# Eight slots instead of nine in the second attention's weighing, and another share of the softmax sums

## What is computed

```python
q = layernorm(q_x, ln_q_g, ln_q_b) @ Wq.T
kv = layernorm(kv_x, ln_kv_g, ln_kv_b) @ Wkv.T
attn = softmax(einsum('bhqd,bhkd->bhqk', q, k) * scale)
out = einsum('bhqk,bhkd->bhqd', attn, v)
x = q_x + out @ Wo.T + bo
h = silu(x @ W1.T + b1)
x = x + h @ W2.T + b2
```

## Time and profile before

| | us |
|---|---|
| three runs, median (lowest to highest) | 5529.31 (5528.18 to 5532.56) |
| the profiled execution | 5531.83 |
| its span, first to last instruction | 5529.7 |
| busy: TensorE / VectorE / ScalarE / GpSimd | 5310.5 / 4009.0 / 3173.3 / 2329.5 |
| mean granted TensorE clock | 0.977 of full |

### The profile page before, as it was taken

One profiled execution on the slowest core, in us unless ns is written; L12 is line 12 of the kernel. 1 busy time (PEld: TensorE's weight loads), 2 busy tenths in 40 slices (PEclk: granted clock), 3 DMA queues, 4 the chain that ended last, 5 costly groups with the idle time before them and its releaser, 6 DMA issues. The chain is left out here.

```text
span 5529.7 us, 93901 instructions
## 1 busy us (share of the span) xinstructions
PE 5310.5 (96%) x28684; PEld 3343.9 (60%) x28684; DVE 4009.0 (72%) x6947; ACT 3173.3 (57%) x5792; POOL 2329.5 (42%) x1156
## 2 busy tenths in 40 slices
PE   8989999999699799999999999999999996999999
PEld 7744444444377466666666666666666663787777
DVE  6589999999577688888888888888888885332331
ACT  4258888888433366666666666666666664322222
POOL 0000000000000388888888888888888885000000
PEclk9989999999899799999999999999999998999999
DMA  7521111111343311111111111111111111322220
GB/s 216 129 46 37 39 38 38 38 38 32 112 120 111 102 41 29 40 41 41 36 34 39 42 41 35 34 40 42 41 32 36 41 30 61 114 92 69 92 84 23
DMA packets 329591, 324.44 MB, mean 59 GB/s; under 512 B 185744, under 2 KB 193808, under 8 KB 327184
## 3 DMA queue, kind: packets, MB, share of 16 engines
q1 hardware_dynamic: 329232, 319.92, 21.8%
HBM read 219.18 MB, written 100.53 MB: 58 GB/s over the span
## 5 line engine op out<-in xcount | busy, mean ns | idle before, releaser
L426 DVE TENSOR_REDUCE a_maxes<-a_mscore 128x1 f32<-128x458 f32 (+4 forms) x5376 | 3037.8, 625 | 599.0 <-PE a_mscore L485 566.9
L409 ACT ACTIVATE a_prob<-a_score 128x512 f32<-128x512 f32 x4992 | 2635.7, 598 | 1184.4 <-PE a_score L494 1171.2
L494 PE MATMUL a_score<-a_q,a_k 97*128 97x512 f32 (+1 forms) x4992 | 1975.6, 430 | 11.6 <-ACT a_prob L409 7.9
L485 PE MATMUL a_mscore<-a_k,a_qm 96*128 96x458 f32 (+4 forms) x5376 | 1892.3, 415 | 53.7 <-DMA a_k<-k 52.4
L513 PE MATMUL a_acc<-a_prob,a_v 128*32 128x512 f32 x9984 | 1593.6, 601 | 0.0
L485 PEld LDWEIGHTS a_mscore<-a_k,a_qm 96*128 96x128 f32 (+1 forms) x5376 | 1475.0, 310 | 177.0 <-issue 54.0
L375 POOL TENSOR_TENSOR a_added<-a_added,a_prob 128x1024 f32<-128x1024 f32 x640 | 1527.3, 2386 | 71.0
L494 PEld LDWEIGHTS a_score<-a_q,a_k 97*128 97x128 f32 (+1 forms) x4992 | 916.0, 193 | 966.5 <-ACT a_prob L409 524.8
L372 POOL TENSOR_TENSOR a_added<-a_prob 128x1024 f32<-128x1024 f32 x128 | 305.1, 2383 | 1893.5 <-ACT a_prob L409 1879.6
L508 PE MATMUL a_acc<-a_prob,a_ones 128*1 128x512 f32 x2048 | 960.9, 591 | 0.0
L513 PEld LDWEIGHTS a_acc<-a_prob,a_v 128*32 128x32 f32 x9984 | 291.8, 108 | 297.7 <-issue 153.2
(11 more groups left out here) (205 smaller groups left out, 3878.0 us busy)
## 6 DMA issues: line engine op xcount, KB each, us to landing
a_qm<-q SPq DMA_DIRECT2D x384, 64.0 KB, 1.9
a_q<-q SPq DMA_DIRECT2D x384, 64.0 KB, 1.9
acc<-a_acc_sb SPq DMA_DIRECT2D x384, 64.0 KB
e_part<-acc SPq DMA_DIRECT2D x90, 256.0 KB, 3.4
a_k<-k SPq DMA_DIRECT2D x48, 416.0 KB, 6.2
q<-m_qout SPq DMA_DIRECT2D x128, 128.0 KB, 2.3
e_wo<-wo_split SPq DMA_DIRECT2D x32, 512.0 KB, 4.1
k<-kv_k1out SPq DMA_DIRECT2D x24, 512.0 KB, 2.9
```

The costliest lines, as they stand in the source:

```text
L409: act.activation(prob[:, t], score[SCORES[it.j][t]][:], ACT.Exp, scale=SCALE).then_inc(exp_done, 1)
L426: dve.tensor_reduce(maxes[j][:, t, c:c + 1], mscore[u % UNIT_BANKS][:, 0:wide], AX.X, ALU.max).then_inc(unit_read, 1)
L485: pe.matmul(mscore[u % UNIT_BANKS][:, 0:wide], qm[j][r:r + ROW, t:NB:NB // P], kt[kk][r:r + ROW, at:at + wide], start=True, stop=True).the ...
L494: pe.matmul(score[SCORES[it.j][t]][:], kt[it.k][r:r + C, i * P:(i + 1) * P], qt[it.j][r:r + C, :], start=True, stop=True).then_inc(score_d ...
```

## The change

- Slots 0 and 1 of an item now hold four value tiles (tiles 0 to 7). Slots 2 to 7 hold three value tiles (8 to 25) and in column 3 a sum: tiles 8, 9, 23, 24, then `rest`, which is the two real rows of tile 25 by `ones[0:2]`, then `total`. That is eight slots in four batches, behind t = 10, 12 (previous item), 17 and 22.
- Column 3 now has two contents in an item: values of batch 0, then sums from batch 1. So ScalarE copies the values of column 3 to a new buffer `side` at t = 20 (`copy_side`), batch 1 waits for that, and SP stores it as a fourth part.
- VectorE adds up tiles 1 to 7, in four pieces of 128 columns (each a strided reduction of 128 by 7 by 128), at t = 8, 10, 12 and 21 of the same item. Piece 0 waits for all of GpSimd's adds of the item before.
- GpSimd adds tiles 0 and 10 to 11 and 12, then pairs 13 to 22: six adds from tile 12's exponential on. The two-row add goes.
- `acc` is copied out at t = 13. The units per tile follow another table.
- `ending` loads and adds four parts. To make room for that, `total` is kept in `h[1]` and some reciprocals in `h[0]`.

```diff
-            self.ROWS, self.SIDE, self.SUMS = 128, 3, 1
-            self.slots = [[(0, 3 * i), (1, 3 * i + 1), (2, 3 * i + 2), (3, ("one", 3 * i))] for i in range(8)]
-            self.slots.append([(0, 24), (1, 25), (3, ("sum", None))])
-            self.batches = [[0, 1], [2, 3], [4, 5], [6, 7], [8]]
-            self.at = {3: (3, True), 9: (4, True), 14: (0, False), 19: (1, False), 25: (2, False)}
-            self.copy_at = 5
+            self.ROWS, self.SIDE, self.SUMS = 128, 4, 1
+            self.slots = [[(c, 4 * i + c) for c in range(4)] for i in range(2)]
+            for i in range(2, 8):
+                first = 8 + 3 * (i - 2)
+                what = [("one", 8), ("one", 9), ("one", 23), ("one", 24), ("rest", 25), ("sum", None)][i - 2]
+                self.slots.append([(0, first), (1, first + 1), (2, first + 2), (3, what)])
+            self.batches = [[0, 1], [2, 3], [4, 5], [6, 7]]
+            self.at = {10: (2, True), 12: (3, True), 17: (0, False), 22: (1, False)}
+            self.copy_at, self.side_at = 13, 20
+            self.sum_at = (8, 10, 12, 21)
...
-            more = dict(enumerate([2, 1, 1, 0, 1, 2, 1, 1, 1, 0, 1, 2, 1, 1, 1, 1, 1, 2, 1, 1, 1, 1, 2, 1, 1, 0]))
+            more = dict(enumerate([1, 2, 1, 0, 2, 0, 1, 2, 1, 1, 0, 2, 0, 1, 1, 2, 1, 1, 1, 1, 2, 1, 1, 2, 0, 1]))
...
-ADDS = 9
-ON_VECTOR, PIECES = range(22, 25), 4
-READ_BY = 7
+ADDS, READ_BY, SUMS_READ = 8, (1, 2, 5, 6), 8
+ON_VECTOR, PIECES = (range(1, 8),), 4
+VSUMS = len(ON_VECTOR) * PIECES
...
+                if APART:
+                    sp.wait_ge(side_copied, n + 1)
+                    sp.dma_start(acc_out[ATEND, bass.ds(h * hd, hd), cols], side[3 * 32:P, :]).then_inc(side_stored, 16)
...
+            def copy_side(n):
+                act.wait_ge(pv_done, n * NBATCH + 1)
+                act.wait_ge(side_stored, n * 16)
+                act.activation(side[3 * 32:P, :], acc[3 * 32:P, :], ACT.Copy).then_inc(side_copied, 1)
...
+                    dve.wait_ge(exp_done, n * ST + tiles[-1] + 1)
+                    if which == 0 and not first:
+                        dve.wait_ge(add_done, n * ADDS - ADDS + SUMS_READ)
...
+                if b == 1 and APART:
+                    pe.wait_ge(side_copied, n + 1)
...
+                            keys = LAST_KEYS if what[0] == "rest" else P
...
-                            mm = pe.matmul(acc[c * 32:c * 32 + 1, :], ones[:],
-                                           total[:] if what[0] == "sum" else prob[:, what[1]],
+                            mm = pe.matmul(acc[c * 32:c * 32 + 1, :], ones[0:keys],
+                                           total[:] if what[0] == "sum" else prob[0:keys, what[1]],
```

More of the change, by code:

```diff
@@ L126, in __init__ @@
         self.opens = {min(ts): b for b, ts in enumerate(tiles)}
-        self.closes = [max(ts) for ts in tiles]
+        summed = [[t[1] for i in b for _, t in self.slots[i] if isinstance(t, tuple) and t[0] != "sum"]
+                  for b in self.batches]
+        self.closes = [max(ts + ones) for ts, ones in zip(tiles, summed)]
         self.units_at, made = [], 0
@@ L385, in _ @@
                 pool.tensor_tensor(total[:], added[:, 0], added[:, 1], ALU.add).then_inc(add_done, 1)
[L386 to L388 removed]
+                pool.wait_ge(vsum_done, it.n * VSUMS + VSUMS)
+                pool.wait_ge(add_done, base + 7)
+                pool.tensor_tensor(total[:], total[:], vsum[:, 0], ALU.add).then_inc(add_done, 1)
         @block.scalar
@@ L403, in exp @@
                     if APART:
-                        last = min(max(L.batches[b][-1], 1), READ_BY - 1)
-                        act.wait_ge(add_done, it.n * ADDS - ADDS + (last if b < NBATCH - 1 else READ_BY))
-                if APART and t == ON_VECTOR[0] and not it.first:
-                    act.wait_ge(vsum_done, it.n * PIECES)
+                        act.wait_ge(add_done, it.n * ADDS - ADDS + READ_BY[b])
+                if APART and t == ON_VECTOR[0][0] and not it.first:
+                    act.wait_ge(vsum_done, it.n * VSUMS)
                 act.activation(prob[:, t], score[SCORES[it.j][t]][:], ACT.Exp, scale=SCALE).then_inc(exp_done, 1)
+            def copy_side(n):
+                act.wait_ge(pv_done, n * NBATCH + 1)
+                act.wait_ge(side_stored, n * 16)
+                act.activation(side[3 * 32:P, :], acc[3 * 32:P, :], ACT.Copy).then_inc(side_copied, 1)
             for it in items(act):
-                for s in range(GROUPS):
-                    if s == L.copy_at and not it.first:
+                for t in range(ST):
+                    if t == L.copy_at and not it.first:
                         copy_acc(it.n - 1, 1 - it.j, it.prev_use)
-                    exp(it, 2 * s)
-                    exp(it, 2 * s + 1)
+                    if APART and t == L.side_at:
+                        copy_side(it.n)
+                    exp(it, t)
                 if it.last:
@@ L461, in _ @@
                             maximum(it.n + 2, it.j, it.use + 1, u)
-                    if APART and t < PIECES and not it.first:
-                        add_up(it.n - 1, t)
-                if APART and it.last:
-                    for i in range(PIECES):
-                        add_up(it.n, i)
+                    if APART and t in L.sum_at:
+                        add_up(it.n, it.first, *divmod(L.sum_at.index(t), PIECES))
             if weights:
@@ L503, in weigh @@
                     for c, what in L.slots[i]:
-                        after = [x for later in L.slots[i + 1:] for x, _ in later if x == c]
+                        kind = lambda x: isinstance(x, tuple)
+                        same = [j for j, slot in enumerate(L.slots) for x, w in slot if x == c and kind(w) == kind(what)]
+                        start, stop = i == same[0], i == same[-1]
                         if isinstance(what, tuple):
+                            keys = LAST_KEYS if what[0] == "rest" else P
                             if what[0] == "sum":
                                 pe.wait_ge(add_done, n * ADDS + ADDS)
-                            mm = pe.matmul(acc[c * 32:c * 32 + 1, :], ones[:],
-                                           total[:] if what[0] == "sum" else prob[:, what[1]],
-                                           start=(i == 0), stop=not after)
+                            mm = pe.matmul(acc[c * 32:c * 32 + 1, :], ones[0:keys],
+                                           total[:] if what[0] == "sum" else prob[0:keys, what[1]],
+                                           start=start, stop=stop)
                             continue
@@ L513, in weigh @@
                         mm = pe.matmul(acc[c * 32:c * 32 + 32, :], vt[kk][:, L.FIRST[half] + at, :],
-                                       prob[:, what], start=(i == 0), stop=not after)
+                                       prob[:, what], start=start, stop=stop)
                 mm.then_inc(pv_done, 1)
@@ L1196, in ending @@
         h = [sb(f"h{i}", [P, NB], F32) for i in range(2)]
+        total = h[1]
+        assert H * T // P == NB
         hh = [sb(f"hh{i}", [P, NB], F32R) for i in range(2)]
@@ L1222, in part_of, with recip_part @@
             return part, 0, 2 + (n - 1) * KT + k
+        def recip_part(n, k):
+            return h[0][:] if n == 0 and k % 2 else part[:, SIDE]
         @block.sync
```

47 lines of the change are left out of this document (20 added, 27 removed).

## The result

The changed kernel takes 5740.85 us (median of 4 runs, 5734.65 to 5743.61) where the kernel before takes 5530.94 (4 runs, 5528.18 to 5536.17) on the same chip: a ratio of 1.0376, with 95% interval 1.036 to 1.0391. It is slower by 210 us. The forecast was slower by 29 (5560), the range ended at 5595.

What follows compares the result with a forecast made beforehand. TensorE was taken to bound each item (21.66 us). Per item -1.16 + 0.86 + 0.2 + 0.3 = +0.2, by 127 items +25, with the ending +31: 5562.8, set as 5560; range 5410 to 5595.

Steps and rivals of the forecast that it cites:

- VectorE's piece: Each of VectorE's four sums an item grows from 384 to 896 elements: 586 ns becomes 1.13 us, 2.2 us more an item.
- It is hidden as a total.: VectorE, at 19.9 us of an item of 20.5 to 22, stays covered, with pieces 0 to 2 just ahead of batches.
- Slot 6: Its two-row fourth matmul among 128-row neighbours was taken to run alone: 0.86 + 0.2 = 1.06 us more an item.
- the high end: Upper bound for slot 6's two-row matmul: run alone with two changes of form, 1.06 us; the low end was 0.
- Rival one: Slot 6's two-row matmul overlaps its neighbours: 0.86 us an item less, 5426 us in all (5405 to 5450); chance 0.33.
- The ninth slot and the fifth batch: Dropping both from TensorE's item saves 1.16 us; four value tiles in a slot cost nothing more.
- Stalls: TensorE's waits, mainly for VectorE's maxima in fourteen scores without a batch: net 0.3 us more an item (0 to 0.5).
- The side copy: ScalarE's copy of column 3 at t = 20 (0.6 us), needed by TensorE only at t = 22: cost 0.
- Rival two: Slot 6 overlaps and VectorE's piece 0 waits for GpSimd, up to 0.5 us an item: 5490 us; chance 0.07.
- The ending: Fourth part's adds and load ahead of the first output product, plus GpSimd's later last chain: 6 us, bounds 2 to 12.
- The other 28 hide beside matmuls: In the ending, the fourth part's extra adds for 28 of 32 tiles cost nothing beside TensorE's matmuls.
- GpSimd's chain of the last item: It starts later and so adds 2 us ahead of the ending.

Runs made afterwards that it cites:

- both repairs: The changed kernel with slot 6's fourth matmul over all 128 rows and VectorE's sum over three tiles instead of seven; 5508.91 us (0.9955).
- the moved order: The changed kernel, 128-row matmul in slot 6, three-tile sum, batches behind tiles 5, 12, 18, 25: 5482.05 us; side copy moved to tile 19 too: 5439.51.
- e_full_rest: The changed kernel with slot 6's fourth matmul over all 128 rows of tile 25, by a second column of ones; 5847.03 us (1.0571).
- a_moved: The changed kernel with batches behind tiles 5, 12, 18, 25 and the side copy ahead of tile 19's exponential; 6135.0 us (1.109).
- v_pairs: The whole kernel with two groups of three tiles, but VectorE adds pairs of tiles as GpSimd does, inside the batches; 5797.49 us (1.0484).

## Why the prediction was wrong

- **VectorE's piece: the step that failed.** "586 + 512 x 1.07 = 1.13 us" took the slope of a reduce over a row for a strided one. The piece is 1.75. The prediction set 1.5 as the point from which VectorE would be the bound, gave that case no chance of its own, and it is what happened. Cutting the sum to three tiles gives 98 us back. Those pieces take 0.59 and not 1.13, so 98 is the price of the whole excess over a short sum; no kernel with pieces of 1.13 was run.
- **"It is hidden as a total."** This fell with it. Four pieces of 1.68 and 28 maxima of 0.54 are about 22 us, against 19.9 in the prediction, and the item is 22.98. With slot 6 repaired and the full clock it is still 23.14.
- **Slot 6: right.** 1.07 against 1.06 forecast. The choice of the high end was right, and the Trainium skill's rule on changing the tiling mode (TensorEngine Tiling (Array Packing), Key Properties) agrees with the runs, for 64 rows as for two. Rival one's premise, that the matmul overlaps, did not hold. The kernel before with one such matmul confirms it (+0.96 an item).
- **The ninth slot and the fifth batch: right.** Four-value batches take 1.85, slots with 128-row neighbours 0.86.
- **Stalls: right in kind, off in size and in cause.** The forecast has 0.56 us an item over TensorE's distances (0.26 and 0.3). The kernel with both repairs shows 0.96. VectorE in the long stretch was counted; missing was the item's first score. Its bank is that of tile 24, two scores back, and no batch stands between them any more. The same row in the changed kernel:

```profile
3022.95 0.50 PE L511 MATMUL a_score<-a_q,a_k 97*128 97x512 f32 x1 [0.25 <-ACT a_prob L419]
```

  This score starts 0.61 us behind the maximum ahead of it (3022.34), where 0.21 is usual. The side copy, costed at nothing, was the other miss: its move was worth 0.33 us an item in the moved order. How much of the 0.96 each of them has in the order of the change was not measured apart.
- **Rival one** said 5426. With both repairs, which make its case true and take VectorE out of the way, the kernel takes 5508.91. Of the 83 us between, 51 are the stalls (0.4 by 127) and 21 the ending; 11 are left.
- **Rival two: false.** VectorE waits for GpSimd at the sum for 10.9 us in the whole run.
- **The ending: half right.** Ahead of the first product the prediction had +4, measured are +0.8; taking the fourth part out there brings 45.01 down to 40.18, so it does cost 4.8, nearly all by its load (44.69 with only the add left out), and 4 us come back in a way that was not traced. "The other 28 hide beside matmuls" failed as well: +27.3 behind the first product, of which 21 are shown to be the fourth part. GpSimd's chain of the last item leaves TensorE waiting 11.04 us instead of 5.94, 5 where 2 was said.
- **The sum of the misses.** The item is 1.12 over the forecast's 21.86, 142 us for 127 of them. Of these 98 went with the sum's length. The other 44 are still there with the short sum, in its 22.20 against 21.86, and are put down to the stalls above. The ending's 27 and 3 for GpSimd's last chain, less 3 ahead of the first product, make 169 of the 181 us between 5560 and 5740.85; 12 are left.

## What to carry to other kernels

Cost an operation from a row with its own access pattern: a slope from contiguous rows did not hold for strided ones, and one measured step (three to four) made more than half of the miss. When a forecast names the value at which the bound would move to another engine, and the row behind that value is not of the same form, that case deserves a chance of its own. A late producer in front of TensorE can cost more than its lateness, so look at the granted clock behind each idle time. Placing long pieces inside TensorE's batches did not help by itself (5844.82 with three of four there); cutting them short and not putting three in front of the busiest tiles did (5467.11).

## What the runs showed of the hardware

- A VectorE reduce of 128 strided sums: 0.58 us over three elements, 1.05 over four, then about 0.2 for each more; seven in a row 1.06, seven strided 1.64 at every distance from 512 to 4096 bytes.
- A matmul on 2 or 64 rows among 128-row neighbours runs alone and adds 0.96 us (2 and 64 rows, last slot of a batch) or 1.07 (2 rows, within one) to a slot of 0.86.
- The clock can fall to half behind TensorE's short waits, and the length of the wait alone does not decide it. In e_full_rest 1.20 us (3007.27) is followed by 0.66 over 4 us and 1.19 us (3031.68) by 1.00. In a_moved 1.35 us is followed by 0.50, which is 1.2 GHz, over two stretches of 6 us together. In v_pairs 0.84 us (3015.99) is followed by 1.00 over 10 us and 0.96 us (3038.40) by 0.61 over 4 us. What decides was not varied. From 2200 to 4400 us these kernels have 0.96, 0.91 and 0.94 on the mean; the changed kernel, where the longest such wait is 0.5, has 1.00.
- A VectorE add with two SBUF inputs and a GpSimd add exclude each other: 1.21 against 2.54 us, and 2.39 against 3.18. A VectorE reduce beside GpSimd shows no such thing.
